# A transformer layer with routed experts on one core: the experts' 176 inner rows split 128 + 48 instead of 88 + 88, with other turns around the router, the opening and the last norm

## What is computed

```python
q, k, v = (ln(x) @ (codes * scales) + b for each of q, k, v)      # 256 -> 2048
attn = softmax(q @ k.T / sqrt(128)); a = (attn @ v) @ (wo_codes * wo_scales) + bo
x = x + ln(a)
p = softmax(ln(x) @ Wr); top 2 of 8, renormalised                 # the router
h = silu(ln(x) @ Wg[e]) * (ln(x) @ Wu[e]);  y = h @ Wd[e]         # per chosen expert e
x = x + ln(sum of weight * y)
```

## Time and profile before

| | |
|---|---|
| runs | 2030.54, 2031.3, 2035.19 us |
| the profiled execution | 2032.58 us, of which 2030.8 us are the span |
| mean granted TensorE clock | 0.984 of full speed |
| PE, DVE, ACT, POOL busy | 1954.3 us (96%), 1757.2 (87%), 1421.6 (70%), 1514.7 (75%) |
| chain that ended last | PE 71%, SP's queue 9%, DVE 6%, POOL 6%, ACT 4%, DMA 2%, issue 2% |

### The profile page before, as it was taken

The page is one execution under the profiler, slowest core; times in us unless marked ns, Lnnn a source line. Parts: engine busy times, 40 slices in busy tenths (PEclk is TensorE's granted clock), DMA queues, the critical chain, the costliest instruction groups (busy, mean ns, idle before and its releaser), DMA issues.

```text
span 2030.8 us, 33350 instructions
## 1 busy us (share of the span) xinstructions
PE 1954.3 (96%) x10978; PEld 1694.6 (83%) x10978; DVE 1757.2 (87%) x2715; ACT 1421.6 (70%) x2686; POOL 1514.7 (75%) x1311
## 2 busy tenths in 40 slices
PE   6999999999999999999999999999999999996993
PEld 5888888888888888888888888888888888886893
DVE  6889889898889889898889889998989879998756
ACT  5777667776767767777677667776777767775565
POOL 2679778797779778787778778887778768896324
PEclk8999999999999999999999999999999999997996
DMA  4677776786667767676677666776667666783454
GB/s 97 156 169 173 174 170 156 163 192 156 161 159 187 176 148 176 155 178 152 144 161 174 156 142 162 166 177 145 152 156 177 156 145 147 164 203 101 129 158 142
DMA packets 173041, 322.68 MB, mean 159 GB/s; under 512 B 47686, under 2 KB 105798, under 8 KB 172870
## 3 DMA queue, kind: packets, MB, share of 16 engines
q1 hardware_dynamic: 169798, 312.15, 65.2%
q0 software_dynamic: 3072, 8.39, 1.3%
HBM read 35.68 MB, written 18.35 MB: 27 GB/s over the span
## 4 chain that ended last, share of the span: by engine, by line
PE 71%; SPq 9%; DVE 6%; POOL 6%; ACT 4%; DMA 2%; issue 2%; POOLq 0%; ACTq 0%
PE ps_a L756 17%; PE ps_s L628 12%; PE ps_s L629 11%; PE ps_s L630 11%; PE ps_a L757 9%; SPq L408 8%; POOL pT_both L531 4%; PE ps_a L628 2%; PE ps_a L629 2%; PE ps_a L630 2%; ACT probs L1074 2%; DVE part_max L1442 1%; DVE probs L1467 1%; DMA pT<-probs 1%; ACT pT_both L1091 1%
## 5 line engine op out<-in xcount | busy, mean ns | idle before, releaser
L531 POOL TENSOR_TENSOR pT_both<-pT,pT_both 128x512 fp32r<-128x512 f32 x1016 | 1289.3, 1300 | 340.8 <-ACT pT_both L1091 338.4
L1074 ACT ACTIVATE probs<-ps_s,shift 128x1024 f32<-128x1024 f32 x512 | 565.9, 1108 | 283.6 <-DVE shift L1451 283.5
L756 PE MATMUL ps_a<-pT_both,v_both 128*128 128x512 f32 x2048 | 745.4, 397 | 0.7 <-POOL pT_both L531 0.6
L1091 ACT ACTIVATE pT_both<-pT 128x512 fp32r<-128x512 f32 x1016 | 605.6, 629 | 160.3 <-DMA pT<-probs 126.7
L1467 DVE STREAM_TRANSPOSE probs<-probs 128x1024 f32<-128x1024 f32 x508 | 613.8, 1228 | 55.1 <-ACT probs L1074 54.5
L1442 DVE TENSOR_REDUCE part_max<-ps_s 128x1 f32<-128x1024 f32 x512 | 612.1, 1215 | 20.5 <-PE ps_s L630 20.3
L757 PE MATMUL ps_a<-pT_both,v_both 128*128 128x256 f32 x2048 | 574.8, 281 | 0.0
L756 PEld LDWEIGHTS ps_a<-pT_both,v_both 128*128 128x128 f32 x2048 | 385.6, 188 | 85.9 <-POOL pT_both L531 1.3
L628 PE MATMUL ps_s<-kT_hi,qT_hi 128*128 128x512 f32 x1024 | 406.4, 397 | 11.5 <-ACT probs L1074 8.4
L629 PE MATMUL ps_s<-kT_lo,qT_hi 128*128 128x512 f32 x1024 | 402.7, 393 | 0.0
L630 PE MATMUL ps_s<-kT_hi,qT_lo 128*128 128x512 f32 x1024 | 401.6, 392 | 0.0
(11 more groups left out here) (216 smaller groups left out, 2551.6 us busy)
## 6 DMA issues: line engine op xcount, KB each, us to landing
pT<-probs SPq DMA_DIRECT2D x2032, 128.0 KB, 2.4
x_rows<-zeros SPq DMA_DIRECT2D x46, 128.0 KB, 2.2
xg<-x_rows SPq DMA_DIRECT2D x46, 128.0 KB, 2.2
y_rows<-y_sb SPq DMA_DIRECT2D x46, 128.0 KB, 2.4
pT<-in_L_attn_x SPq DMA_DIRECT2D x4, 512.0 KB, 5.7
codes<-in_L_attn_wk_codes SPq DMA_DIRECT2D x16, 128.0 KB, 2.4
scales<-in_L_attn_wk_scales SPq DMA_DIRECT2D x64, 32.0 KB, 3.0
codes<-in_L_attn_wo_codes SPq DMA_DIRECT2D x16, 128.0 KB, 2.3
```

Of the source, the lines that this page charges most:

```text
L531: pool.tensor_tensor(pT_lo[:, p, :].rearrange("p (i n) -> p i n", i=Q4), pT[:, s % 2, :, g, t:t + 2, :].rearrange("p i t q -> p i (t q)"), ...
L756: nc.tensor.matmul(out_both, v_hi[:, h % 2, k, :], move, start=k == 0, stop=False)
L1074: nc.scalar.activation(out, src, ACT.Exp, bias=shift[:, s % SLOTS, r:r + 1], scale=SCALE, accum_out=sums[:, s % SLOTS, r, g:g + 1])\
L1091: nc.scalar.activation(pT_hi[:, p, :].rearrange("p (i n) -> p i n", i=Q4), pT[:, s % 2, :, g, t:t + 2, :].rearrange("p i t q -> p i (t q)" ...
```

## The change

- The inner rows are split 128 + 48. The second group is stacked: `hid` gets 256 columns a seat, of which 176 are the rows, 192 to 239 the last 48 rows again (a second DVE product), and the rest zero (`hid` is moved to the end of SBUF, a POOL memset clears columns 176 on once). Turned, partitions 0 to 47 and 64 to 111 of the second group hold the same rows; the second half of `d_hi` has Wd's high part at 0 to 47 and its low part at 64 to 111. One matmul over 112 rows gives high x high and high x low, one over 48 rows gives low x high: five matmuls a seat instead of six. Wd comes in four DMAs instead of two.
- `turn_last(2)` and `turn_last(3)` come later in PE's order, `route(0)` earlier.
- Part 0's logits no longer wait for the moments of tiles 10 and 11, which DVE takes after `seat_experts(0)`.
- `route(1)` has three identity transposes between tiles and six ahead; 24 and 8 behind it become 8 and 6. DVE does `tie_broken(1)` and `choose(1)` in seats 0 and 1, with the later steps of part 1's choice one seat further on, and `count_all(1)`, `count_places(1)` on PE in seats 2 and 3.
- Opening: PE transposes the identity five times at each of several waits (`warm_up`); chunk 3's norm moves from ACT to DVE; the last k projection is split after its first 512 columns (`k_half`).
- End: batches 8, 4, 2, 1, 1; from tile 8 on DVE subtracts the mean while ACT takes the root, then one DVE operation scales and adds the residual; the constant part of the first norm is added to x1 earlier, in seats 14 to 29 (`add_base`); the epsilon is ACT's bias; `weigh` waits for the first gathered row alone; the last two tiles are stored one by one.

```diff
@@ constants
-    KD = I // 2
+    KB = I - P
+    KS = P // 2 + KB
-    BATCHES = [(0, 8), (8, 4), (12, 2), (14, 2)]
+    BATCHES = [(0, 8), (8, 4), (12, 2), (14, 1), (15, 1)]
+    FIRST = BATCHES[0][1]
@@ PE, opening
+            def warm_up(name, value, n):
+
+                pe.wait_ge(sm[name], value)
+                for _ in range(n):
+                    nc.tensor.transpose(ps_a[:, 0, 0:P], ident[:, :], ident[:, :])
+
+            for t in range(1, TPC):
+                warm_up("xn_done", t, 5)
             turn_tiles(xn_in, 0, "xn_done", "xn_t", "xT_lo_done")
+            for t in range(TPC + 2, 2 * TPC):
+                warm_up("xn_done", t, 5)
+            warm_up("xT_hi_done", 1, 5)
             turn_tiles(xn_in, 1, "xn_done", "xn_t", "xT_lo_done")
...
@@ PE, the loop over n
                 weighted_values(n - 2, 1)
+                if n == LAST + 2:
+                    turn_last(TU - 1)
...
                 out_proj(n - 3)
-                weighted_values(n - 2, 3)
-                if n == LAST + 1:
-                    turn_last(2)
-                scores(n + 1, 1, 0)
-                weighted_values(n - 2, 4)
                 if n == LAST + 2:
                     wait(pe, "last_lo", PAIRS_KT)
                     route(0)
+                weighted_values(n - 2, 3)
+                scores(n + 1, 1, 0)
+                weighted_values(n - 2, 4)
...
                 weighted_values(n - 1, 0)
+                if n == LAST + 1:
+                    turn_last(2)
@@ PE, route and down
+                    if u == 1 and a < n - 1:
+                        keep_running(3)
...
-                for k in range(2):
-                    hi, lo = hs_hi[0:KD, j % 3, k * P:(k + 1) * P], hs_lo[0:KD, j % 3, k * P:(k + 1) * P]
...
-                    last = product3(ps_y(j), hi, lo, w_h, w_l, first=k == 0, last=k == 1)
+                a_hi, a_lo = hs_hi[:, j % 3, 0:P], hs_lo[:, j % 3, 0:P]
+                b_hi, b_lo = hs_hi[0:KS, j % 3, P:2 * P], hs_lo[0:KB, j % 3, P:2 * P]
+                product3(ps_y(j), a_hi, a_lo, w_of_seat(d_hi, P, 0), w_of_seat(d_lo, P, 0), last=False)
+                nc.tensor.matmul(ps_y(j), b_hi, w_of_seat(d_hi, KS, 1), start=False, stop=False)
+                nc.tensor.matmul(ps_y(j), b_lo, w_of_seat(d_hi, KB, 1), start=False, stop=True)\
...
@@ PE, before the seats
             turn_rows(3)
+            keep_running(6)
             route(1)
-            keep_running(24)
+            keep_running(8)
             turn_x(0, 0)
             turn_x(0, 1)
-            keep_running(8)
+            keep_running(6)
@@ DVE
-                V.tensor_tensor(hid[:, j % 3, :], silu_g[:, j % 2, :], ps_gate(j)[:, I:2 * I], ALU.mult)\
-                    .then_inc(sm["h_done"], 1)
+                V.tensor_tensor(hid[:, j % 3, 0:I], silu_g[:, j % 2, :], ps_gate(j)[:, I:2 * I], ALU.mult)
+                V.tensor_tensor(hid[:, j % 3, 3 * P // 2:P + KS], silu_g[:, j % 2, P:I], ps_gate(j)[:, I + P:2 * I],
+                                ALU.mult).then_inc(sm["h_done"], 1)
...
+            def add_scaled_residual(t):
+
+                dve.wait_ge(sm["centred"], t - FIRST + 1)
+                dve.wait_ge(sm["x1_based"], t + 1)
+                V.scalar_tensor_tensor(x1[:, t, :], ysum[:, t % YR, :], rstd3[:, t:t + 1], x1[:, t, :],
+                                       ALU.mult, ALU.add).then_inc(sm["out_ready"], 1)
```

More of the change, by code:

```diff
@@ L255, in sandwich_layer @@
         pT_loaded = [sem(f"pT_loaded{g}") for g in range(NG2)]
-        res_loaded = [sem(f"res_loaded{g}") for g in range(NCH)]
         gu_loaded = [sem(f"gu_loaded{c}") for c in range(DC)]
@@ L263, in sandwich_layer @@
         y_stored = [sem(f"y_stored{b}") for b in range(YS)]
-        yg_loaded = [sem(f"yg_loaded{b}") for b in range(GR)]
+        yg_loaded = [[sem(f"yg_loaded{k}{b}") for b in range(GR)] for k in range(2)]
         block = ctx.enter_context(nc.Block())
@@ L485, in _ @@
                     store_seat(n - 9)
-            for t in range(0, TT, 2):
-                store_out(t)
-            sp.wait_ge(sm["out_stored"], 16 * (TT // 2))
+            for t in range(0, TT - 2, 2):
+                store_out(t, 2)
+            store_out(TT - 2, 1)
+            store_out(TT - 1, 1)
+            sp.wait_ge(sm["out_stored"], 16 * (TT // 2 + 1))
         @block.gpsimd
@@ L589, in _ @@
             gate_up_lo(1)
+            wait(pool, "pv_done", PAIRS_KT * HALVES)
+            pool.memset(hid[:, :, I:2 * P], 0.0).then_inc(sm["const_done"], 1)
             def send(u):
@@ L819, in _ @@
             q_proj(0)
+            for t in range(2 * TPC + 2, 3 * TPC):
+                warm_up("xn_done", t, 5)
+            warm_up("xT_hi_done", DC + 1, 5)
             turn_tiles(xn_in, 2, "xn_done", "xn_t", "xT_lo_done")
@@ L862, in _ @@
                 weighted_values(n - 2, 6)
-                if n == LAST + 1:
-                    turn_last(TU - 1)
                 weighted_values(n - 2, 7)
@@ L949, in turn_h @@
                     wait(pe, "hs_lo_done", j - 1)
-                last = nc.tensor.transpose(ps_h(j)[:, k * P:(k + 1) * P], hid[:, j % 3, k * KD:(k + 1) * KD],
+                last = nc.tensor.transpose(ps_h(j)[:, k * P:(k + 1) * P], hid[:, j % 3, k * P:(k + 1) * P],
                                            ident[:, :])
@@ L1053, in _ @@
             input_std(3)
-            input_norm(3)
             input_hi(2)
@@ L1225, in _ @@
                 if n == LAST:
-                    nc.scalar.activation(warm, zero[:, :], ACT.Sqrt).then_inc(sm["warm_done"], 1)
+                    nc.scalar.activation(warm, zero[:, :], ACT.Sqrt)
                 probs_hi(n - 1, 0)
@@ L1325, in out_std @@
                 run = slice(BATCHES[b][0], sum(BATCHES[b]))
-                act.wait_ge(sm["eps3"], b + 1)
-                nc.scalar.activation(std3[:, run], std3[:, run], ACT.Sqrt).then_inc(sm["std3_done"], 1)
+                act.wait_ge(sm["eps_set"], 1)
+                act.wait_ge(sm["aggr3"], sum(BATCHES[b]))
+                nc.scalar.activation(std3[:, run], mv3[:, run, 1], ACT.Sqrt, bias=eps_col, scale=1.0)\
+                    .then_inc(sm["std3_done"], 1)
             def out_norm(t):
-                act.wait_ge(sm["shift3_done"], 1 + max(b for b in range(len(BATCHES)) if BATCHES[b][0] <= t))
+                act.wait_ge(sm["shift3_done"], 1)
                 nc.scalar.activation(ysum[:, t % YR, :], ysum[:, t % YR, :], ACT.Identity,
@@ L1409, in input_scale, with input_norm @@
                     .then_inc(sm["shifted_done"], 1)
+            def input_norm(c):
+                for t in range(TPC * c, TPC * (c + 1)):
+                    V.tensor_scalar(xn_in[:, t, :], x_in[:, t, :], mv[:, t, 0:1], rstd[:, t:t + 1],
+                                    ALU.subtract, ALU.mult).then_inc(sm["xn_done"], 1)
             def input_lo(c):
@@ L1867, in hidden_lo @@
                 dve.wait_ge(sm["hs_hi_done"], j + 1)
-                V.tensor_tensor(hs_lo[0:KD, j % 3, :], ps_h(j), full(hs_hi[0:KD, j % 3, :]), ALU.subtract)\
+                V.tensor_tensor(hs_lo[:, j % 3, :], ps_h(j), full(hs_hi[:, j % 3, :]), ALU.subtract)\
                     .then_inc(sm["hs_lo_done"], 1)
             def combine(t):
+                dve.wait_ge(yg_loaded[1][t % GR], 16 * (t // GR + 1))
                 dve.wait_ge(sm["ysc_done"], t + 1)
@@ L1928, in _ @@
             down_lo(0, 0)
+            down_lo(0, 4)
             sum_logits(1)
@@ L1939, in _ @@
                 if n == 0:
-                    down_lo(0, 4)
+                    tie_broken(1)
                 if n == 1:
+                    choose(1)
                     down_lo(1, 0)
-                    seat_starts(1)
                 if n == 2:
                     down_lo(1, 4)
+                    seat_starts(1)
+                if n == 3:
                     seat_rows()
-                if n == 3:
+                if n == 4:
                     take_places(1)
                     rows_of(1)
-                if n == 4:
+                if n == 5:
                     seat_experts(1)
@@ L1955, in _ @@
                     weights_of(1)
+                if n >= 14 and n - 14 < TT:
+                    if n == 14:
+                        dve.wait_ge(xn2_done[0], sum(DVE_FROM))
+                    add_base(n - 14)
                 if n in POST:
@@ L1963, in _ @@
             out_scale(0)
-            out_shift(0)
-            for t in range(8):
+            out_shift()
+            for t in range(FIRST):
                 add_residual(t)
```

176 lines of the change are left out of this document (100 added, 76 removed).

## The result

The changed kernel takes 2043.96 us (median of 5 executions, 2042.83 to 2047.41) where the kernel before took 2030.57 (5 executions, 2030.17 to 2035.19). One later execution of the kernel before took 8101 us, where the twelve beside it took 2028 to 2037, and is left out of the ratios. The profiled execution took 2044.56 us, its span is 2042.5, 11.7 more than the profiled span before. The table further down splits these 11.7 us by stage.

A forecast was written before the change was run, and what follows sets the result against it. PE was taken to bound attention and the seats, chains through several engines the rest. Terms -2.7 - 1.2 + 0.1 - 0.2 + 1.7 - 5.2 - 2.4 = -9.9 us gave 2021.4 us (-0.5%), range 2017.3 to 2027.7.

The forecast's parts named there:

- item 5: Down products in the seats: five matmuls instead of six, 44 products saved at 0.118 us each, -5.2 us.
- rival A: Down products: changing the rows in use drains PE, 0.25 us a change, +23 us, result 2044; chance 7%.
- Item 2: Transition after attention: first half, later last turns free ACT's high parts, -1.2 us; second half, earlier `route(0)`, 0.
- Item 1: Opening: warm-ups hold the clock, chunk 3's norms on DVE, last k projection split, -2.7 us.
- rival B: Opening, transition and `route(1)`: the warm-ups do not hold the clock, 3.3 us worse, 2024.7; chance 11%.
- Item 3: Into the seats: `xs_lo` takes the tie row's place, -2.5, transposes in `route(1)` delay logits, +2.4; -0.2 us.
- Item 4: First seats: PE waits for DVE, which gains tie and choice steps and `hid` products, +1.7 us.
- rival C: Seats: not bound by PE once six products are five, so the down products save nothing, 2026.6; chance 9%.
- Item 6: End, behind the gathers: weighing waits for one row only and DVE steps drop out, -2.4 us.

The follow-up runs named there:

- the first run: The changed kernel with the last down product of each seat over 112 rows instead of 48: 2029.33 us, ratio 0.9987 to the kernel before.

## Why the prediction was wrong

**The step that failed is item 5**: "I take it that a product over 112 or 48 rows costs what one over 88 does, since the same 256 columns pass". For 112 rows that is right, for 48 it is not. Instead of -5.2 us, seats 5 to 45 gave +10.0 and the last three down products +0.6. Worked out from the steps, 46 seats save a product (5.4) and pay two changes of 0.20 us each (18.4), +13.0; the first run, which takes the changes away, gave back 14.3. This is rival A, with chance 7%, and by its own point of decision (0.11 us a change) it had to win. Its price was taken as 0.25 between ends of 0.16 and 0.35 (the 0.16 and the weight load's 0.14 of the earlier trace rows make only 0.30); 0.20 was measured. That its 2044 us is so near the measured 2043.96 is partly luck: its 23 us for the changes are 4.6 too many, and `route(0)` and a slower attention made up for them. Of its two arguments the one that was put against it was wrong: going from 128 to 88 rows costs nothing visible, but that was no evidence, since both are over 64. The nearest row wasn't near: no product of the trace was on the other side of the limit. The rule of the Trainium skill (page TensorEngine Tiling (Array Packing), section Key Properties: a change of tiling mode drains the engine) agrees with the runs: 32, 48 and 64 rows paid, 65, 96 and 112 did not. The runs show the price and its limit; that what is paid is a drain they don't show. Rival A should have had most of the chance, because nothing in the trace spoke against it for this size.

**Item 2, second half, was wrong**: for `route(0)` ahead of the two pairs I took "the same PE work in another order. I take 0, at best -1.1", with no end above zero. It was +3.1 us (9.23 to 12.38) in the changed kernel and +1.6 in the four other kernels with this order; against the order put back, 1.9. The work is the same, but with `route(0)` first five pairs stand behind it instead of three, they fall into the stretch at low clock, and `choose(0)` waits for them. The trace of before had shown a fall behind `route(0)` too (0.85 from 1858 to 1860 us), and I used it for `route(1)` alone. The first half agrees in the changed kernel: the turned rows came 1.3 us sooner behind attention, forecast 1.2. In the four other kernels with this order it was 0.3 to 1.6, so the closeness is in part luck. ACT's fifth high part began at 1843.70; said was "near 1842", to which attention's 1.9 us come. (Pair 3 stood ahead of `turn_last(2)` in the kernel before already; the turns stood ahead of pairs 4 to 7 only.)

**Item 1 was right**: -2.88 for -2.7 (the range of item 1 went from -3.6 to -1.2). The clock stood at 1.00 from 12 to 24 us, so rival B fell, and the warm-ups are worth 1.8. Of the Trainium skill's sentence (TensorE: Matmul & The Clock Gate, Part 4: PE-mode transpose) that the full clock doesn't engage for transposes, the run without warm-ups shows the opposite again (0.50 from 14 us on without the 45 transposes, 1.00 with them). But "a start that comes sooner moves everything behind it" held for the sum only within what attention itself varies: 1.9 us of the 2.9 were gone by its end.

**Item 3** (-0.2; its own terms, -2.5 and +2.4, make -0.1) gave +0.05. In it the 21 transposes cost 2.1 us (2.4 said), the tie steps gave 2.0 (2.5 said; ACT's `xs_hi` became last). **Item 4** (+1.7) gave +2.18, of which 0.67 is the price of the changes of height: 1.5 without them.

**Item 5 without the 48 rows** is what the first run shows: 2.00 us a seat at best, 0.12 less than the best seats before (2.10 to 2.12), but 83.06 / 40 = 2.08 on average where 2.02 was said. PE starts late now and then, as from 1971.79 to 1974.19, where one seat took 2.40: its down product began 0.33 us behind the last gate product, where 0.16 is usual, and the profile names no engine for it (its weight load stands "0.29 <-issue"). `hs_lo` had been there since 1971.94. So the seats fell short as rival C has it, but only in part, with 2.7 us for the forty and not 4.7, and what holds PE up stays open.

**Item 6** (-2.4) gave -2.6 behind the last gather (7.05 to 4.46): 0.9 ahead of the last `combine` (0.6 said), and 1.7 from there on (1.8 said, though the add that stood in between was tile 13's, 0.31 to the next start, and not tile 14's). From PE's last product to the end of the span it is also 2.6 (32.71 to 30.10), but 1.0 to 2.8 in the ten runs with the same end (31.66 to 29.95). Outside the seats one term was missing altogether: the 76 transposes behind `base_done`, from which the forecast took its proof for the clock, ran at low clock until about 1880 us, and the turns behind them started 0.5 late.

With 112 rows and `route(0)` put back, the stages outside attention sum up to 238.21 us (2024.7 - 1786.49) against 245.54, -7.3 where -9.9 had been said; most of the difference is the 2.2 us that the forty seats fell short of.

## What to carry to other kernels

Before a contraction is split unevenly, look whether a piece has 64 rows or fewer among pieces with more: each change of height, in and out, cost 0.20 us here, more than a whole product of 256 columns (0.12), and filling the piece up to over 64 rows with zeros or with a term that does no harm cost nothing. PE's busy share stays at 100% while this goes on; only the distance from start to start shows it. Behind small products the clock was often low in these traces, so dense ones that something waits for are better put ahead of them, when there is a choice (1.1 to 1.9 us here). And a rule that the trace cannot test is not refuted by rows from its safe side.
